# Two-layer cross-attention with a routed FFN: the mask's exchange behind the stack transfers, pieces and small operations on other engines

## The reference

```
x = x + attention0(norm(x), ctx)     # 16 heads of 8, rotary, no mask
x = x + ffn0(norm(x))                # quantized weights, 128 -> 512 -> 128, relu
x = x + attention1(norm(x), ctx, mask)  # 16 query heads, 4 key/value heads,
                                     # causal and given mask, norm of the output
x = x + moe(norm(x))                 # 8 experts, top 1: gelu, 128 -> 512 -> 128, times gate score
```

## Time and profile before

| | us |
|---|---|
| median of 3 runs | 588.3 |
| profiled execution | 586.95 |
| its span in the trace | 585.1 |
| TensorE busy with matmuls | 495.1 (85%) |
| VectorE / GpSimd / ScalarE busy | 399.3 / 374.8 / 357.0 |
| TensorE's granted clock, mean | 0.978 |

### The profile page before, as it was taken

The page is one execution under the profiler, slowest core; times in us unless marked ns, Lnnn a source line. Parts: engine busy times, 40 slices in busy tenths (PEclk is TensorE's granted clock), DMA queues, the critical chain, the costliest instruction groups (busy, mean ns, idle before and its releaser), DMA issues.

```text
span 585.1 us, 20027 instructions
## 1 busy us (share of the span) xinstructions
PE 495.1 (85%) x6238; PEld 363.5 (62%) x6239; DVE 399.3 (68%) x1244; ACT 357.0 (61%) x872; POOL 374.8 (64%) x751
## 2 busy tenths in 40 slices
PE   3569898999988799988799999899998742999993
PEld 2346566666665589986455555555554422999992
DVE  7657777777798568644668888888878763444441
ACT  3227677777766555653566777677765652666661
POOL 6876666667673257675666688878887472445552
PEclk9999999999999999999999999999999985999998
DMA  5734334353432580004443455444554014334430
GB/s 165 184 76 125 90 92 118 85 126 87 119 89 64 193 226 1 1 2 111 118 111 89 104 134 137 128 103 111 133 138 110 26 56 143 80 96 104 101 94 27
DMA packets 102161, 59.92 MB, mean 102 GB/s; under 512 B 20338, under 2 KB 98178, under 8 KB 102098
## 3 DMA queue, kind: packets, MB, share of 16 engines
q1 hardware_dynamic: 98738, 51.79, 35.1%
q0 software_dynamic: 2784, 6.82, 3.4%
q10 hardware_dynamic: 576, 0.53, 0.3%
HBM read 19.90 MB, written 8.81 MB: 49 GB/s over the span
## 4 chain that ended last, share of the span: by engine, by line
PE 47%; SPq 14%; DVE 10%; DMA 10%; issue 10%; ACT 4%; POOL 3%; ACTq 1%; DVEq 0%; POOLq 0%
SPq L395 8%; DMA stack<-pieces 7%; PE bank L847 6%; PE bank L783 5%; PE bank L669 5%; PE scoreT L773 4%; DVE negmax L1408 4%; PE scoreT L835 4%; PE score L613 4%; PE bank L556 2%; PE score L835 2%; SPq L404 2%; PE bank L528 2%; PE scoreT L642 2%; PE bank L684 2%
## 5 line engine op out<-in xcount | busy, mean ns | idle before, releaser
L1408 DVE TENSOR_REDUCE negmax<-score 128x8 f32<-128x1024 f32 x128 | 156.2, 1220 | 35.4 <-PE score L613 24.9
L956 ACT ACTIVATE P<-scoreT 128x1024 f32<-128x1024 f32 x128 | 131.0, 1023 | 40.1 <-PE scoreT L633 21.7
L669 PE MATMUL bank<-P,Vc 128*32 128x128 f32 x2048 | 82.5, 279 | 1.9 <-DVE product L1516 1.5
L613 PE MATMUL score<-stack 64*128 64x128 bf16 x1024 | 62.7, 222 | 22.1 <-DMA stack<-pieces 13.1
L1312 POOL DMA_INDIRECT out<-by x39 | 40.2, 1031 | 50.6 <-DVE by L1715 48.0
L613 PEld LDWEIGHTS score<-stack 64*128 64x128 bf16 x1024 | 33.9, 95 | 48.7 <-issue 22.1
L669 PEld LDWEIGHTS bank<-P,Vc 128*32 128x32 f32 x2048 | 48.4, 109 | 15.8 <-issue 3.6
L962 ACT COPY outs<-bank 128x256 f32<-128x256 f32 x64 | 23.6, 369 | 49.8 <-PE bank L669 49.6
L1176 POOL TENSOR_TENSOR pieces<-full,pieces 128x256 bf16<-128x256 f32 x64 | 42.9, 670 | 14.4 <-ACT pieces L937 14.4
L1179 POOL TENSOR_TENSOR pieces<-rest,pieces 128x256 bf16<-128x256 f32 x64 | 43.8, 685 | 5.0
L847 PE MATMUL bank<-M,bhT 128*128 x312 | 43.5, 282 | 0.3 <-ACT bhT L1082 0.3
(11 more groups left out here) (211 smaller groups left out, 1265.7 us busy)
## 6 DMA issues: line engine op xcount, KB each, us to landing
stack<-pieces SPq DMA_DIRECT2D x192, 128.0 KB, 2.8
ctxT<-in_ctxT SPq DMA_DIRECT2D x32, 128.0 KB, 2.5
XB<-expert_rows SPq DMA_DIRECT2D x39, 66.0 KB
XA<-expert_rows SPq DMA_DIRECT2D x39, 64.0 KB
XR<-in_x SPq DMA_DIRECT2D x4, 512.0 KB, 4.5
stack<-blank SPq DMA_DIRECT2D x32, 64.0 KB, 2.1
stack<-negpT SPq DMA_DIRECT2D x64, 32.0 KB, 1.8
M<-in_M SPq DMA_DIRECT2D x1, 2048.0 KB, 9.9
```

The source lines that it names most:

```text
L613: mm = nc.tensor.matmul(SCORE[:, r, i * 128:(i + 1) * 128], Qs[pb][rows, h, tb * S:(tb + 1) * S], Ks[pb][rows, kv, tb * S:(tb + 1) * S], s ...
L669: mm = nc.tensor.matmul(PVOUT[VCOL * i:VCOL * (i + 1), half * 128:(half + 1) * 128], Vc[:, k % BODY, at:at + VCOL], P32[:, c, i * 128:(i + ...
L956: nc.scalar.activation(P32[:, half * 2:half * 2 + 2, :], SCORET[:], ACT.Exp, scale=SCALE).then_inc(sem("exp_done"), 1)
L1408: nc.vector.tensor_reduce(negmax[:, k % 2, :, half * HQ:(half + 1) * HQ], SCORE[:].rearrange("p r (h k) -> p r h k", h=HQ), AX.X, ALU.max, ...
```

## The change

- `stack_both` waits for the high pieces and sends slot 0, waits for the middle ones and sends slots 1, 2, 4, waits for the low ones and sends 3 and 5. In both layers. Before it waited once, for all pieces.
- In layer 1 `swap_mask` moves from the end of the even step to the odd step, behind `stack_both` and `max_rows`, ahead of `load_ctx` and `load_adj`. Its pair is the same.
- In layer 1 the middle piece is cast by ScalarE from the float32 rest (`middle`, behind the step's second exponential). GpSimd makes the rest alone, and the low piece later in the step (`cut_low`). In the even step its row write is moved ahead of `out_rstd` and `add_bias`.
- GpSimd computes the mean's shift in two operations in `mean_rstd`; VectorE's `mean_shift` goes.
- VectorE's `choose` is cut in two; `choose_first` (the first one of equals) runs in the next odd step behind the first maxima, from tile 32 on in the same step as before.

The diff, without a hunk that only renames `rest` to `other_relus` on ScalarE:

```diff
@@ -35,6 +35,7 @@
 SLOTS = len(QSLOT)
+SLOT_ORDER = (0, 1, 2, 4, 3, 5)
 STRIDE = 8
@@ -387,11 +388,17 @@
                     if is_pair(p):
-                        cut_q, cut_k = known(3 * (p + P0) + 3), known(3 * (p + P0) + 3)
-
-                        sp.wait_ge(sem("q_pieces"), cut_q)
-                        sp.wait_ge(sem("k_pieces"), cut_k)
-                        for s in range(SLOTS):
+                        high, middle, low = known(p + P0 + 1), known(3 * (p + P0) + 1 + L), known(3 * (p + P0) + 3)
+
+                        sp.wait_ge(sem("q_high"), high)
+                        sp.wait_ge(sem("k_high"), high)
+                        for s in SLOT_ORDER:
+                            if s == SLOT_ORDER[1]:
+                                sp.wait_ge(sem("q_pieces"), middle)
+                                sp.wait_ge(sem("k_pieces"), middle)
+                            if s == SLOT_ORDER[4]:
+                                sp.wait_ge(sem("q_pieces"), low)
+                                sp.wait_ge(sem("k_pieces"), low)
                             sp.dma_start(rows_of(stack[b], s), both_pieces(b, s)).then_inc(sem(f"stacked{L}{b}"), 16)
@@ -417,11 +424,11 @@
                     if j % 2 == 1:
+                        if L:
+                            swap_mask(j + 3)
                         load_ctx(j + 7)
...
                             load_adj(j + 5)
-                    if L and j % 2 == 0:
-                        swap_mask(j + 4)
@@ -936,6 +943,14 @@
+                def middle(k, which):
+
+                    p = pair(k)
+                    if is_pair(p):
+                        nm = "qk"[which]
+                        act.wait_ge(sem(f"{nm}_pieces"), 3 * (p + P0) + 1)
+                        nc.scalar.copy(pieces[turn(k)][:, 3 * which + 1, :], rest[which][:]).then_inc(sem(f"{nm}_pieces"), 1)
+
                 def values(k):
@@ -1024,6 +1039,11 @@
                         if j % 2 == 0:
+                            middle(j + 4, 1)
+                        else:
+                            middle(j + 5, 0)
+                    if L:
+                        if j % 2 == 0:
                             whole(j + 6, 0)
@@ -1173,10 +1193,18 @@
                         pool.wait_ge(sem(f"{nm}_high"), p + P0 + 1)
-                        nc.gpsimd.tensor_tensor(pc[:, 1, :], f, h, ALU.subtract).then_inc(sem(f"{nm}_pieces"), 1)
+                        if L == 0:
+                            nc.gpsimd.tensor_tensor(pc[:, 1, :], f, h, ALU.subtract).then_inc(sem(f"{nm}_pieces"), 1)
                         nc.gpsimd.tensor_tensor(r, f, h, ALU.subtract).then_inc(sem(f"{nm}_pieces"), 1)
+
+                def cut_low(k, which):
+
+                    p = pair(k)
+                    if is_pair(p):
+                        nm = "qk"[which]
+                        pc = pieces[turn(k)][:, 3 * which:3 * which + 3, :]
                         pool.wait_ge(sem(f"{nm}_pieces"), 3 * (p + P0) + 2)
-                        nc.gpsimd.tensor_tensor(pc[:, 2, :], r, pc[:, 1, :], ALU.subtract).then_inc(sem(f"{nm}_pieces"), 1)
+                        nc.gpsimd.tensor_tensor(pc[:, 2, :], rest[which][:], pc[:, 1, :], ALU.subtract).then_inc(sem(f"{nm}_pieces"), 1)
@@ -1219,6 +1247,10 @@
                         nc.gpsimd.tensor_tensor(rs, rs, powers[:, 0:2], ALU.pow).then_inc(sem("m_rstd"), 1)
+                        pool.wait_ge(sem("m_rstd"), 2 * u + 2)
+                        nc.gpsimd.tensor_tensor(mshift[:, tiles], mmv[:, tiles, 0], rs, ALU.mult).then_inc(sem("m_centred"), 1)
+                        pool.wait_ge(sem("m_centred"), u + 1)
+                        nc.gpsimd.tensor_tensor(mshift[:, tiles], zero[:, 0:2], mshift[:, tiles], ALU.subtract).then_inc(sem("m_shifted"), 1)
@@ -1239,21 +1271,26 @@
                     if L == 0:
+                        cut_low(k, which)
                         if j % 2 == 0:
...
                             whole(j + 5, 1)
-                    if L:
+                    else:
                         if t == B:
...
                         if j % 2 == 0:
+                            for i in scattered_at(t):
+                                scatter(i)
                             out_rstd((t - 2) // 2)
                             add_bias(j + 4)
+                            cut_low(k, which)
                         else:
                             mean_rstd((t - 5) // 2)
-                        for i in scattered_at(t):
-                            scatter(i)
+                            cut_low(k, which)
+                            for i in scattered_at(t):
+                                scatter(i)
@@ -1483,6 +1520,12 @@
                     nc.vector.bn_aggr(mmv[:, 2 * u + 1, :], mstats[:, 2 * u + 1, :]).then_inc(sem("m_aggregated"), 1)
+
+                def choose_first(u):
+
+                    if not is_pair(u):
+                        return
+                    tiles, r = slice(2 * u, 2 * u + 2), u % TURNS
                     dve.wait_ge(sem("logits_centred"), u + 1)
@@ -1500,14 +1543,6 @@
                     nc.vector.tensor_tensor(sums[:, (u + 1) % TURNS, :], sums[:, r, :], both[:], ALU.add).then_inc(sem("summed"), 1)
-
-                def mean_shift(u):
-
-                    if is_pair(u):
-                        tiles = slice(2 * u, 2 * u + 2)
-                        dve.wait_ge(sem("m_rstd"), 2 * u + 2)
-                        nc.vector.scalar_tensor_tensor(mshift[:, tiles], mmv[:, tiles, 0], -1.0, mrstd[:, tiles], ALU.mult, ALU.mult
-                                                       ).then_inc(sem("m_shifted"), 1)
@@ -1536,10 +1571,10 @@
                     maxima(t + 2, 0, j + 2)
-                    if L and t >= B and j % 2 == 0:
-                        mean_shift((t - 6) // 2)
                     if L and j % 2 == 0:
                         make_mask(j + 4)
+                    if L and j % 2 == 1 and t < B:
+                        choose_first((t - 5) // 2)
                     denominators(t - 1)
@@ -1550,14 +1585,14 @@
                         if j % 2 == 0:
-                            if t < B:
-                                mean_shift((t - 6) // 2)
                             place_of((t - 6) // 2)
...
                             choose((t - 4) // 2)
+                            if t >= B:
+                                choose_first((t - 4) // 2)
                         else:
```

More of the change, by code:

```diff
@@ L1097, in _ @@
             early = attention(1)
-            first_evacs, rest = ffn(early)
+            first_evacs, other_relus = ffn(early)
             body_loop(act, step, START, {B + 1: first_evacs})
-            rest()
+            other_relus()
             body_loop(act, early, EARLY - AHEAD, None, LAST)
```

## The result

The changed kernel takes 600.8 us at the median of 4 runs (596.18 to 603.81), the kernel before beside it 588.9 (587.66 to 589.98): a ratio of 1.020 [1.012, 1.027]. The forecast was 594.0. The direction was right, the loss is twice as large, and the time lies just above the range.

What follows compares the result with a forecast made beforehand. Layer 1 was taken as bound by SyncE's queue, with TensorE waiting for the stack. Terms of 5.0 + 0.8 + 0.4 = 6.2 us on 586.95 gave 593.2; about half of the 1.35 offset made it 594.0, range 585.5 to 600.

Steps and rivals of the forecast that it cites:

- What bounds the kernel: Layer 1 is a loop through SyncE's queue: TensorE idles 0.56 us for the stack in the odd step shown.
- part 1: Exchange moved to layer 1's odd step: TensorE waits for it, 6.62 us after the odd start against 6.36 now.
- To: The odd step's start in a pair of layer 1, 359.87 in the pair shown; the exchange's terms count from it.
- The sum: (6.72 - 6.36) x 14 = 5.0 us for layer 1's pairs, + 0.8 + 0.4 = 6.2 us.
- Part 2: Stack transfers by piece: last issue 0.5 us earlier, a real gain but covered by the exchange's wait.
- Part 3: Middle casts on ScalarE: the even step's exponential and negpT come 0.10 us late, bounds 0 and 0.2.
- Part 4: GpSimd loses two middle pieces a pair and gets two small mean operations, net -0.8 us; priced at 0.
- Part 5: VectorE's three small operations, 0.6 us together, move behind the odd step's first maxima; priced at 0.
- Part 6: Context and mask loads behind the exchange on SyncE's queue come later; 0 to 2 us in all, taken as 0.
- Part 7: Layer 0's split waits add 0.8 us in five pairs; GpSimd's shift at the tail adds 0.4.
- The exchange waits for the burst ahead: Rival: exchange lands in 2.4 us or more instead of 1.8, mask load stalls VectorE; 600 to 604, chance 0.10.
- The stack stall just goes: Rival: exchange lands before the last maxima are done, odd step about 5.86 us; 581 to 582, chance 0.12.

Runs made afterwards that it cites:

- e1: The kernel before with only the mask's exchange moved into the odd step behind the maxima; 598.1 us, ratio 1.015.
- e2: The changed kernel with the exchange put back in the even step, behind the first maxima and ahead of the stack; 588.2 us, ratio 1.000.
- e6: The changed kernel with the exchange back in the even step and GpSimd's odd-step row write ahead of the low cut; 587.9 us, ratio 0.997.
- e9: e6 without the waits by piece, with the slots' order of the kernel before; 601.4 us, ratio 1.025.
- e13: The kernel before with SyncE's steps of layer 1 written out straight instead of a loop; 588.7 us, ratio 1.001.
- e11: The changed kernel with the exchange in the odd step ahead of the second maxima transfer, and GpSimd's row write ahead of the low cut; 588.3 us, ratio 1.000.
- e5: The kernel before with only the stack transfers' waits by piece and the slots' new order; 585.4 us, ratio 0.995.

## Why the prediction was right in direction and too small

- **What bounds the kernel, and part 1: right.** Every term held in a regular pair: maxima issue at To + 3.31 (forecast 3.28), landing 1.79 (1.80), start 0.23 after it (0.32), regular odd steps 6.5 to 6.7 (6.7), pairs 12.5 (12.6), no wait for the stack. e1 shows that this part alone makes most of the loss, e2 that without it there is none.
- **The sum: this step failed.** It multiplied a regular pair's 0.36 by 14 and gave 5.0. Measured is 11.7: the seven regular pairs from tile 8 on add 1.25, that is 0.18 each and half of what was forecast, since these pairs took 12.32 before and not the mean of 12.24, and 12.50 after and not 12.60; six irregular ones add 10.4. The term that was missing is what an unsteady issue costs once it stands on the path. The trace of before had it, unseen by TensorE. Timeline of SyncE's queue, before:

```profile
284.41 2.14 SPq L404 DMA_DIRECT2D swapped<-mask  x2
303.20 1.75 SPq L374 DMA_DIRECT2D adj<-in_mask  x1
```

I read the queue in the pairs that repeat, where almost no code is fetched, and took their 1.22 as the price for all. The earlier trace rows too had a longest landing of 3.7 for the maxima, and I used its 1.8.

- **The granted clock: not in the sum.** Before it was 1.00 in all of these pairs; each of the three slow issues was followed by an even step 1.0 to 1.4 longer than before. No part asks what a longer idle time of TensorE does.
- **Part 2: half right.** The gain is covered, as said. But in e6, where the exchange is out of the way, it is more than the 0.5 priced, and without it part 3 is a loss of 13.5 us (e9). The timing was right: the last stack issue of the pair from 374.89 goes out 7.9 after the even start (forecast 8.1, before 8.6).
- **Part 3: right here** (ScalarE's delay is not to be seen in regular pairs). **Part 4 was priced at 0 and that held only under the exchange's wait.** I looked at where the split of the odd step would start, and not at that of the even one behind the row write; e2 and e6 show that this order costs 0.7 a pair once nothing else is late. GpSimd is 15.0 us less busy and ScalarE 8.9 more, where 12 each were forecast.
- **Part 5: not tried alone.** TensorE's waits for the maxima are as long as before (8.3 us in all), which agrees with its 0.
- **Part 6: right.** No wait of VectorE for the mask load appears (before there was one, of 0.58).
- **Part 7: can't be told.** Tile 2 stands at 281.97 against a forecast of about 282.0, but with layer 0's code unchanged it stands at 278.65 in e1 and 279.98 in e13. The same holds for the end: +2.6, of which the forecast had 0.4, while e1 and e13, with the tail of before, have 133.9 and 134.1 against 132.46.
- **The rivals.** "The exchange waits for the burst ahead" named 600 to 604 and so the right time, by a wrong mechanism: the landing was 1.79, not 2.4. "The stack stall just goes" lies where e6 and e11 get in six pairs, and only with GpSimd's order changed.

## What to carry to other kernels

A transfer with a whole step to spare also absorbs what isn't in the average: before it is moved to where a consumer waits for it, look for the longest issue on its queue in the straight parts of the program, not for the median in the loop. When such a wait grows to 2 us, count TensorE's lower clock behind it as well; here it fell behind most of them. And an engine's order that is free today is free only under the wait that covers it; check it again for the case in which that wait is gone. The fastest version here was the smallest edit, e5 (0.995 [0.991, 0.999]).

## What the runs showed of the hardware

Fetching TensorE's code shows in the DMA view as single packets of 16 KB on a queue of kind instruction, 7 to 14 us apart in straight code between 283 and 358 us and hardly one while a loop of six steps repeats. An issue on SyncE's queue that meets one takes up to 1.4 us longer (the pair of exchange issues 1.7 to 2.5 instead of 1.24; a load 0.95 to 1.85 instead of 0.4). About half of the packets in layer 1 meet an issue in this way.

The granted clock fell to 0.50 behind some idle times of TensorE and not behind others. Counted at the even tiles 2 to 30 of all 16 traces, it fell within 1 us before or 3 us after the start in 15 of 18 cases with an idle time of 2.0 us or more ahead (up to 3.3), in 10 of 20 with 1.5 to 2.0, and in 11 of 202 with less. Nine of these 11 are at tile 2, where 1.05 us of idle time stand ahead in the kernel before as well; why the clock falls there in some executions stays open.
